# Routed experts on sorted tokens: rows scattered by expert, weights picked by register, rows gathered back

## The reference

```python
shared = einsum('bsi,hi->bsh', silu(x @ shared_gate.T) * (x @ shared_up.T), shared_down)
probs = sigmoid(einsum('bsh,eh->bse', x, router_w) + routing_bias)
scores, indices = top_k(probs, 2)
scores = scores / sum(scores)
w = zeros((t, 8)).at[arange(t)[:, None], indices].add(scores)
g = silu(einsum('th,ehi->tei', xf, gate_w))
u = einsum('th,ehi->tei', xf, up_w)
combined = einsum('tei,eih,te->th', g * u, down_w, w)
return shared + combined
```

## Time and profile before

| | |
|---|---|
| median of 3 runs | 948.55 us (947.72 to 948.93) |
| profiled execution | 948.73 us, its span 946.5 us |
| mean granted TensorE clock | 0.948 |
| busy: PE, PEld, DVE | 854.0, 562.8, 613.4 us |
| busy: ACT, POOL | 526.0, 321.1 us |

### The profile page before, as it was taken

One profiled execution on the slowest core, in us unless ns is written; L12 is line 12 of the kernel. 1 busy time (PEld: TensorE's weight loads), 2 busy tenths in 40 slices (PEclk: granted clock), 3 DMA queues, 4 the chain that ended last, 5 costly groups with the idle time before them and its releaser, 6 DMA issues. The chain is left out here.

```text
span 946.5 us, 16760 instructions
## 1 busy us (share of the span) xinstructions
PE 854.0 (90%) x5342; PEld 562.8 (59%) x5342; DVE 613.4 (65%) x1838; ACT 526.0 (56%) x914; POOL 321.1 (34%) x452
## 2 busy tenths in 40 slices
PE   6466999999999999999999986659999999999996
PEld 6342555454545455454545445657888888888884
DVE  4976676666766676666766615857666666666665
ACT  3321666666666566666666562226565555555554
POOL 2130121211212121211212123406666666666664
PEclk9775999999999999999999999659999999999999
DMA  8000000000000000000000000005514434544503
GB/s 207 0 1 0 2 2 2 2 1 2 1 2 2 2 3 1 2 1 3 1 1 2 2 2 1 0 27 78 102 39 87 66 76 78 70 73 78 77 2 89
DMA packets 52672, 28.11 MB, mean 30 GB/s; under 512 B 4297, under 2 KB 52577, under 8 KB 52609
## 3 DMA queue, kind: packets, MB, share of 16 engines
q1 hardware_dynamic: 52608, 27.29, 15.7%
HBM read 24.93 MB, written 2.36 MB: 29 GB/s over the span
## 5 line engine op out<-in xcount | busy, mean ns | idle before, releaser
L598 ACT ACTIVATE p_sb<-bank,inv_scale 128x512 f32<-128x512 f32 (+1 forms) x384 | 222.1, 614 | 130.8 <-PE bank L538 127.7
L641 DVE CUSTOM_DVE_ANT_0 junk<-bank,causal 128x512 bf16<-128x512 f32 (+3 forms) x512 | 224.5, 484 | 71.9 <-PE bank L520 71.9
L493 POOL TENSOR_SCALAR_AFFINE_SELECT p_sb<-p_sb 128x384 f32<-128x384 f32 x128 | 66.6, 520 | 404.2 <-ACT p_sb L598 404.2
L1073 DVE TENSOR_TENSOR gu<-bank,sg 128x512 f32<-128x512 f32 x144 | 99.5, 691 | 100.3 <-ACT sg L1018 100.3
L537 PE MATMUL bank<-ql,ah 128*128 128x512 f16 (+3 forms) x512 | 153.4, 300 | 0.0
L538 PE MATMUL bank<-qh,al 128*128 128x512 f16 (+3 forms) x512 | 152.9, 300 | 0.0
L520 PE MATMUL bank<-ah,qh 128*128 128x512 f16 (+3 forms) x512 | 135.8, 310 | 15.6 <-DVE low L641 11.5
L617 DVE TENSOR_TENSOR ql<-bank,qh 128x512 f16<-128x512 f32 x128 | 88.5, 692 | 92.1 <-ACT qh L590 92.1
L536 PE MATMUL bank<-qh,ah 128*128 128x512 f16 (+3 forms) x512 | 147.1, 300 | 0.0
L944 POOL TENSOR_TENSOR gul<-gu,guh 128x512 fp32r<-128x512 f32 x72 | 98.6, 1370 | 139.0 <-DVE yw L1063 107.7
L1018 ACT ACTIVATE sg<-bank 128x512 f32<-128x512 f32 x144 | 86.3, 599 | 104.7 <-PE bank L986 104.1
(11 more groups left out here) (165 smaller groups left out, 1238.5 us busy)
## 6 DMA issues: line engine op xcount, KB each, us to landing
wbc<-w_dram SPq DMA_DIRECT2D x8, 2048.0 KB, 28.8
wst<-in_Wkqv SPq DMA_DIRECT2D x8, 264.0 KB, 5.0
x_sb<-in_x SPq DMA_DIRECT2D x8, 256.0 KB, 5.9
out<-x_sb SPq DMA_DIRECT2D x8, 256.0 KB, 2.4
wraw<-in_gate_w SPq DMA_DIRECT2D x8, 128.0 KB, 27.9
wraw<-in_up_w SPq DMA_DIRECT2D x8, 128.0 KB, 10.3
wraw<-in_down_w SPq DMA_DIRECT2D x8, 128.0 KB, 8.9
c_dram<-lowT SPq DMA_DIRECT2D x32, 4.0 KB, 1.3
```

Of the source, the lines that this page charges most:

```text
L598: nc.scalar.activation(p_sb[v % P_RING][:, S_AT[k]:S_AT[k] + S_WIDTH[k]], m.psum[S_BANK[k]][:, 0:S_WIDTH[k]], ACT.Exp, scale=m.inv_scale[: ...
L641: last = nc.vector.tensor_tensor_reduce(out=junk[:, (3 * u + k) % 2, at:at + w], in0=m.psum[M_BANK[(3 * u + k) % 2]][:, at:at + w], in1=m. ...
L1073: nc.vector.tensor_tensor(gu[par][:, k, :], m.psum[UB[k]][:, :], sg[:, k, :], ALU.mult).then_inc(gu_ready, 1)
```

## The change

The dense sweep over eight experts is replaced by one over sorted rows; the shared expert stays dense.

- `prepare` no longer splits the shared weights, and makes small tables on POOL (triangles, expert equality, tile starts, powers of 8).
- `attention`: SP first fills the new DRAM buffers `xs_dram` with zeros (5.1 MB, six DMAs), then, beside the last groups, loads each expert's weights once; DVE takes their absolute maxima (nine reductions of 128x768), from which a scale for each kind of weight is made in a short chain, with one small matmul across partitions.
- `route` is the former `after_attention`. SP loads all expert weights (3.1 MB) into SBUF. ACT makes scaled float16 high parts `wh` of all of them. The token parts `xh`, `xl` are float16, scaled by 8. The normed rows `hn` are kept. The chain on DVE goes on: `picked` marks the chosen experts, TensorE counts them within and before each tile with small matmuls, and DVE works out for both choices of every token a slot (`place`), for every slot tile its expert (`tile_expert`, eight three-bit numbers in one word) and the two weights. Each half of the tokens (`SPLITS`) has its own slots; each expert's run starts at a full tile, so a half needs at most 39 tiles.
- `experts`: POOL scatters the rows of `hn` to `xs_dram` with 64 indirect DMAs (128 rows each), first half first. TensorE meanwhile does the shared expert (16 units: a sequence and a half k). Then come the slot tiles, two to a unit, up to four to a load (`Quad`): SP loads them, TensorE transposes, ACT and DVE split, and TensorE multiplies with `wh` and `wl` at a row that it reads from a register (`value_load`, `snap`). The down product now has the activations as weights and the expert's matrix as the moving side, so it comes out by token. ACT copies the result and stores it to `ys_dram` on its own queue. When a half is stored, POOL gathers it back with 32 indirect DMAs; DVE multiplies by the two weights and adds to x; SP stores.
- The DVE writes the low parts `wl` of the routed weights during the shared expert (three operations of 128x2048).

The core of the diff:

```diff
@@ attention, sync
+            for g, n in enumerate(SLOT_TILES):
+                for first in range(0, n, 13):
+                    some = min(13, n - first)
+                    sp.dma_start(m.xs_dram[g][first * P:(first + some) * P, :].rearrange("(j p) d -> p j d", p=P),
+                                 m.causal[:, 0:D].unsqueeze(1).to_broadcast([P, some, D])).then_inc(zero_filled, 16)
             for g in range(GROUPS):
+                if 0 <= (e := g - W_GROUP) < E:
+                    if e >= 2:
+                        sp.wait_ge(w_max_ready, e - 1)
+                    sp.dma_start(wraw[:, e % 2, 0:I], m.gate_w[e, :, :]).then_inc(w_loaded[e % 2], 16)
...
@@ attention, vector
+                e, r = divmod(t - W_AT, GROUP)
+                if 0 <= e <= E and r == 0:
+                    if e < E:
+                        dve.wait_ge(w_loaded[e % 2], 48 * (e // 2 + 1))
+                    weights = wraw[:, e % 2, :] if e < E else m.shared_raw[:, :]
+                    nc.vector.tensor_reduce(out=m.w_max[:, e, :], in_=weights.rearrange("p (k i) -> p k i", k=KINDS), axis=AX.X, op=ALU.max, apply_absolute_value=True).then_inc(w_max_ready, 1)
@@ route, sync
+            sp.dma_start(m.raw[:, 0, :, :], m.gate_w.rearrange("e h i -> h e i")).then_inc(raw_loaded, 16)
...
@@ route, scalar
+            def split_high(k):
+                act.wait_ge(raw_loaded, 64)
+                nc.scalar.activation(m.wh[:, :].rearrange("p (e w) -> p e w", w=EW)[:, 0:E, k * I:(k + 1) * I], m.raw[:, k, :, :], ACT.Copy, scale=m.w_scale[:, k:k + 1]).then_inc(wh_ready, 1)
@@ route, vector, at the end of the chain
-            c.link(nc.vector.tensor_tensor(eq[:, :, :], sel[:, 0, :, :], sel[:, 1, :, :], ALU.add))
-            c.link(nc.vector.tensor_tensor(eq[:, :, :], eq[:, :, :], pr[:, :, :], ALU.mult))
+            nc.vector.tensor_tensor(picked[:, :, :], sel[:, 0, :, :], sel[:, 1, :, :], ALU.add).then_inc(picked_ready, 1)
...
+            dve.wait_ge(counted, 1)
...
+            dve.wait_ge(ranked, 1)
...
+            c.link(nc.vector.tensor_reduce(out=slot[:, :, :].rearrange("p k t -> p (k t)"), in_=chosen[:, :, :, :].rearrange("p k t e -> p (k t) e"), axis=AX.X, op=ALU.add))
+            nc.vector.tensor_copy(m.place[:, :, :], slot[:, :, :])
@@ experts, gpsimd
+            for g, (t0, t1) in enumerate(SPLITS):
+                for t in range(t0, t1):
+                    for k in range(2):
+                        nc.gpsimd.indirect_dma_start(out=m.xs_dram[g], out_offset=bass.IndirectOffsetOnAxis(ap=m.place[:, k, t:t + 1], axis=0),
+                                                     in_=m.hn[:, t, :], in_offset=None).then_inc(rows_sent[g], 16)
+            for g, (t0, t1) in enumerate(SPLITS):
+                for k in range(X_RING):
+                    pool.wait_ge(ys_stored[k], 16 * stores_before(g, k))
+                for t in range(t0, t1):
+                    for k in range(2):
+                        nc.gpsimd.indirect_dma_start(out=yg[:, t, k, :], out_offset=None, in_=m.ys_dram[g],
+                                                     in_offset=bass.IndirectOffsetOnAxis(ap=m.place[:, k, t:t + 1], axis=0)).then_inc(fetched[t // TB], 16)
@@ experts, tensor
+            def expert(quad, a):
+                w, i = divmod(quad.first + a, WORD)
+                return pe.snap((words[quad.part, w] >> (3 * i)) & (E - 1), min_val=0, max_val=E - 1)
...
+            def three(bank, at, hi, lo, x_h, x_l):
+                out = bank[:, at:at + x_h.shape[-1]]
+                nc.tensor.matmul(out, hi, x_h, start=True, stop=False)
+                nc.tensor.matmul(out, hi, x_l, start=False, stop=False)
+                return nc.tensor.matmul(out, lo, x_h, start=False, stop=True)
...
+                    for a in range(n):
+                        row = tile_row(quad, a0 + a)
+                        cols = slice((a0 + a) * P, (a0 + a + 1) * P)
+                        x_h, x_l = xsh[:, quad.q % X_RING, cols], xsl[:, quad.q % X_RING, cols]
+                        for k in range(2):
+                            for kind, bank in ((0, GB), (1, UB)):
+                                at = bass.ds(row + (kind * I + k * P), P)
+                                last = three(m.psum[bank[u % 2]], (a * 2 + k) * P, m.wh[:, at], m.wl[:, at], x_h, x_l)
...
+            def down_tile(bank, col, h_of, l_of, w_of):
+                out = bank[:, col:col + D]
                 for k in range(2):
+                    nc.tensor.matmul(out, h_of(k), w_of(m.wh, k), start=(k == 0), stop=False)
+                    nc.tensor.matmul(out, l_of(k), w_of(m.wh, k), start=False, stop=False)
+                    last = nc.tensor.matmul(out, h_of(k), w_of(m.wl, k), start=False, stop=(k == 1))
+                return last
```

More of the change, by code:

```diff
@@ new lines, in _ @@
+            for k in range(2):
+                nc.vector.tensor_tensor(m.weight[:, k, :], top[:, 2 * k, :], top[:, 3, :], ALU.mult)
+            dve.wait_ge(counted, 1)
+            for g, (t0, t1) in enumerate(SPLITS):
+                last = nc.vector.tensor_copy(totals[0:(t1 - t0) * E, g, :], m.psum[6][0:(t1 - t0) * E, g * P:(g + 1) * P])
+            last.then_inc(totals_ready, 1)
+            dve.wait_ge(ranked, 1)
+            counts = m.psum[7][:, PARTS * P:PARTS * P + PARTS * E]
+            n_full = P // E
@@ new lines, in _ @@
+            c.link(nc.vector.tensor_tensor(above[:, :, :, :].rearrange("p g e k -> p (g e) k"), counts.unsqueeze(2).to_broadcast([P, PARTS * E, n_full]),
+                                           m.full_tiles[:, :].unsqueeze(1).to_broadcast([P, PARTS * E, n_full]), ALU.is_gt))
+            c.link(nc.vector.tensor_reduce(out=n_tiles[:, :, :].rearrange("p g e -> p (g e)"), in_=above[:, :, :, :].rearrange("p g e k -> p (g e) k"), axis=AX.X, op=ALU.add))
+            for g in range(PARTS):
+                last = nc.vector.tensor_tensor(stacked[:, g, :, :], n_tiles[:, g, :].unsqueeze(1).to_broadcast([P, E, E]), m.lower_experts[:, :, :], ALU.mult)
@@ L876, in experts @@
[L876 to L897 removed]
+    gu = sb("gu", [P, 2, N], F32)
@@ L899, in experts, with stores_before @@
+    def stores_before(part, k):
+        return sum(1 for quad in quads if quad.part <= part and quad.q % X_RING == k)
     with nc.Block() as block:
@@ L929, in _ @@
+            for quad in quads:
+                load(quad)
+            for b in range(B):
+                sp.wait_ge(out_ready, (b + 1) * TB)
+                sp.dma_start(m.out[b, :, :].rearrange("(t p) d -> p t d", p=P), m.x_sb[:, seg(b, TB), :]).then_inc(out_stored, 16)
             sp.wait_ge(out_stored, 16 * B)
@@ new lines, in _ @@
+            pe.wait_ge(wl_ready, 1)
+            for u in range(UNITS_F + LATE):
+                if u == SHARED:
+                    pe.wait_ge(wl_ready, 1 + KINDS)
+                    for g in range(PARTS):
+                        for w in range(WORDS[g]):
+                            words[g, w] = pe.value_load(m.tile_expert[w:w + 1, g:g + 1], min_val=0, max_val=E ** WORD - 1)
+                if u < UNITS_F:
+                    for quad in to_prepare(u):
+                        transpose(quad)
+                    up(u)
+                if finished(u - LATE) is not None and u - LATE < UNITS_F:
+                    down(u - LATE)
```

557 lines of the change are left out of this document (333 added, 224 removed).

## The result

The kernel after took 970.6 us (median of four runs, 968.2 to 979.7) and the kernel before 948.65 (four runs) on the chip of this comparison: ratio 1.025, 95% interval 1.018 to 1.032. It is slower (whether by more than 2% the interval leaves open), and faster was forecast. The same kernel, run later on a chip called C here beside the kernel before, took 897.6 against 948.8: ratio 0.9465, interval 0.9446 to 0.9485. Both are shown side by side, since the difference between them is the subject. The chips are called X (this comparison), A, B, C, D and E, in order of time; the kernels of one group of experiments shared a chip. A to E are five different chips; which one X was is not on record, so it can be one of these five. The kernel before took 948.1 to 949.4 us (medians) on all of them. A run more than 1.5% above the fastest run of its kernel on that chip is left out of medians and ratios.

What follows compares the result with a forecast made beforehand. TensorE's streamed columns bound the experts' stage. Scatter and first loads to 689.2, 78 tiles at 2.1 us to 853.0, last products, uncovered gathers and stores to 904.8, plus 2.2 gave 907.0 us; range 844 to 975.

Steps and rivals of the forecast that it cites:

- the sum: Whole kernel: stage starts, scatter, 78 routed tiles and uncovered last gathers added up to span 904.8, time 907.0 us.
- rival D: Experts' stage: DVE and GpSimd hold each other up, 8 us on the scatter, 915; within the forecast's shared chance 0.54.
- A: First scatter and last gathers: indirect DMAs serialise at 2.4 us each, giving 984 us; chance 0.13.
- B: Routed tiles: TensorE's sequencer takes 2.7 us a tile, addresses not kept in registers, giving 954 us; chance 0.08.
- C: Routed tiles and indirect DMAs: a tile at 1.5 us and a DMA at 0.8, giving 844 us; chance 0.22.
- Three us for attention: Attention: nine DVE reductions mostly fill idle time, a few delay maxima TensorE awaits; 3 us taken between 0 and 8.6.
- eight for the chain of routing: Routing: the serial DVE chain grows by counts and slots, so the stage ends at 640.8 rather than 632.8.
- the nothings for the zero fill: Start of attention: SP's 5.1 MB zero fill is through by 80 to 91, before it matters, costing nothing.
- rival E: Zero fill: runs at 109 GB/s, 47 us, scores 12 us late, 919; within the forecast's shared chance 0.54.
- the 1.65 from 0.11 and 0.055: Routed tile: 12 pairs (weight load and matmul) with fresh address at 0.11 us, 6 reusing one at 0.055; 1.65 us.
- the 0.1 for the low clock: Routed tile: 0.1 us added for stretches at 1.2 GHz, raising a tile from 2.0 to 2.1 us.
- One reading of before: Experts' stage of the kernel before: 1296 matmuls 0.2275 us apart make 295 us, taken as the stage, so TensorE bounds it.

Runs made afterwards that it cites:

- the gathers-last kernel: Kernel after with one wait changed, so all 64 gathers run after the last store of both halves: 980.95 us (ratio 1.032) on A, 932.6 on C.

## Why the prediction was wrong, and where it was right

**The steps that failed** are two sentences of the sum: the second scatter "lies beside 82 us of routed work: hidden", and the first half's gathers "start near 778 and end by 817, hidden". They cost 36.5 and 37.8 us on X, by comparison with C: the second scatter kept the signal of the first transposes back by 36.3 us, and beside the gathers TensorE started 24 matmuls in 38 us. I had asked whether DVE or ACT would delay GpSimd (rival D), and never whether GpSimd's issuing could delay TensorE, whose signals everything else waits for. No rival had that direction. Of the two slower rivals, A put 984 us on indirect DMAs of 2.4 us, which stand 1.25 apart, so the range held the time of X by luck, for a reason that did not occur; the 979.2 on D lies outside it. B (2.7 us for a tile) and C (1.5, and 0.8 for a DMA) did not occur either.

**The rest of the sum**, on C, where the two sentences hold (the forecast span was 904.8, measured 892.8):

- Start of the scatter: 643.8 forecast, 644.0 measured. Three us for attention, eight for the chain of routing and the nothings for the zero fill (832 KB each, landing after 8.2 us) and the weight loads were right together; rival E did not occur.
- The ten register loads start 0.7 us apart in the sequencer and take 0.30 us each; all ten are through in 6.5 us, where 6 were forecast, and hidden as forecast. Chip C:

```profile
L1219 PEldq TENSOR_LOAD <-tile_expert x10: 296/304/495, 678.4 to 684.6; - x10
```

- First scatter, 38.4 forecast: 644.0 to 690.3, 46.3 us. An indirect DMA takes 0.95 us with 0.30 between, 1.25 where I took 1.2. The other 6 us are rival D (8 us) in the stretch that it named, but by another operation: the four DMAs that meet VectorE's three splits of 2.35 us are 4.8 us longer than 0.95 in all, the others, most of them beside the subtraction `gul` that D counted on, only 1.4. Chip C:

```profile
661.85 2.35 DVE L1278 SCALAR_TENSOR_TENSOR wl<-raw,w_scale,wh 128x2048 f16<-128x2048 f32 x1
662.42 2.62 POOL L1120 DMA_INDIRECT xs_dram<-hn,place  x1 [0.30 <-issue]
```

  The DMA ends at 665.04, 0.84 us after VectorE's split (664.20), as if nearly all of its own 0.95 us had begun only then. The Trainium skill, "SBUF — State Buffer", section "SBUF: two separate sides", says that GpSimd cannot write its descriptors while VectorE holds their shared port; this row agrees. The first routed product stood at 697.3 rather than 689.2.
- Tile, 2.1 us forecast: (834.3 - 697.3) / 78 = 1.76, 27 us less in all. Three products, two of them with a fresh address, start in 0.24 us (chip C below), so 1.42 for a tile's 18 rather than the 1.65 from 0.11 and 0.055. The clock stood at 1.00 in those stages, so the 0.1 for the low clock was not needed.

```profile
800.09 0.23 PE L1185 MATMUL bank<-wh,guh 128*128 x1
...
800.33 0.23 PE L1185 MATMUL bank<-wh,guh 128*128 x1
...
800.57 0.23 PE L1185 MATMUL bank<-wh,guh 128*128 x1
```

- End: the last gathers begin 7.4 us after the last gate and up product is begun (forecast 6.0 after 853.0) and take 43.0 rather than 38.4, since the first takes 4.1 alone; then 8.1 rather than 7.4 to the end. Chip C:

```profile
841.68 4.11 POOL L1127 DMA_INDIRECT yg<-ys_dram,place  x1 [15.64 <-DMA ys_dram<-yst]
846.09 0.95 POOL L1127 DMA_INDIRECT yg<-ys_dram,place  x1 [0.30 <-issue]
...
883.73 0.94 POOL L1127 DMA_INDIRECT yg<-ys_dram,place  x1 [0.30 <-issue]
```

Together: + 8.1 (first product) - 26.8 (tiles) + 1.4 + 4.6 + 0.7 = -12.0, the distance from 904.8 to 892.8. Without the hold-up 907 was 1% too high; with it, 64 us too low. One reading of before is loose: 1296 products at 0.2275 make 295 us, and the stage is 289; nothing in the sum rests on it.

**What stays open.** Whether it is the chip itself, or what else ran beside the kernel on X, A and D, can't be told: D was met twice, some five minutes apart, and had it twice, and none of A to E was seen both with and without it. Of the 1261 signals of TensorE in the experts' stage of the ten kernels on B, C and E none is seen late: two have no record, all others came within 0.02 us. A span was recorded for every run, so whether the hold-up occurs when nothing is recorded isn't shown either. Why TensorE's signals, and then its instructions, are kept back beside an unbroken series, and why the crawl goes in steps of 0.7 us, no run shows; after the last scatter of the gathers-last kernel on A (over at 730.7) the crawl even went on to 736.7, and on X, after the gathers (over at 865.4), to 870.5. Nor was it tried whether less than 0.54 us between two DMAs is enough.

## What to carry to other kernels

Before counting an indirect DMA as hidden, ask what its issuing does to the other engines, and measure it on more than one chip: the same kernel gained 5.4% on C and lost 2.5% on X and 3.2% on D, while the medians of the one before it stayed within 0.2% on all. Before believing that an edit cured something, look in the trace at a stretch that the edit does not touch; if that has changed too, the cure is not the edit. And look at the tail first: 32 gathers with nothing beside them cost 43 us, and moving half of them under the products more than paid for seven more tiles.

## What the runs showed of the hardware

- On some chips or at some times (X, A, D) an unbroken series of indirect DMAs from GpSimd, 1.25 us apart, keeps TensorE's semaphore changes back, at the worst by 40.2 us on X, 45.0 on D and 49.6 on A, and lets matmuls through mostly 0.7 to 2.8 us apart, in steps of 0.7; plain DMAs from GpSimd, 0.54 us each, don't, nor do indirect ones 2.8 us apart, or 1.67 apart with a fill between.
- An indirect DMA of 128 rows of 512 B holds GpSimd for 0.95 us and starts every 1.25; landing takes 2.2 to 2.5. Single ones held it for 4.1 to 8.4.
- Idle work on VectorE lengthens the second scatter, from its first start to its last, from 39.8 to 42.7 us (subtractions of 0.68 us, two inputs) or 41.2 (copies of 0.42); on ScalarE it is 40.0.
- A register load in TensorE's sequencer takes 0.30 us, and ten of them, with what stands between, 6.5.
